# Values' product and output projection one step later, with every step's probabilities turned through memory

## The reference

```python
x = x + tanh(g_xattn[0]) * attention(layernorm(x), ctx)
x = x + tanh(g_ffn[0]) * (moe(layernorm(x)) + shared_ffn(layernorm(x)))

# attention: 32 query heads, 8 key/value heads, head size 128, per batch of 64 rows
q = rmsnorm(h @ Wq.T); k = rmsnorm(ctx @ Wk.T); v = ctx @ Wv.T
probs = softmax(q @ k.T / sqrt(128) + mask)
out = (probs @ v) @ Wo.T
# moe: 16 experts, the best two of each row
```

## Time and profile before

| | |
|---|---|
| median of 3 runs | 1366.95 us (1365.96 to 1368.43) |
| profiled execution | 1367.91 us |
| its span, first to last instruction | 1366.2 us |
| granted TensorE clock, mean | 0.999 |
| steps 4 to 55, from the start of step 4 to that of step 56 | 245.66 to 946.04 us |

### The profile page before, as it was taken

The page is one execution under the profiler, slowest core; times in us unless marked ns, Lnnn a source line. Parts: engine busy times, 40 slices in busy tenths (PEclk is TensorE's granted clock), DMA queues, the critical chain, the costliest instruction groups (busy, mean ns, idle before and its releaser), DMA issues.

```text
span 1366.2 us, 24589 instructions
## 1 busy us (share of the span) xinstructions
PE 1351.8 (99%) x8473; PEld 1092.8 (80%) x8474; DVE 1041.6 (76%) x2190; ACT 505.4 (37%) x1085; POOL 359.9 (26%) x375
## 2 busy tenths in 40 slices
PE   8999999999999999999999999999999999999998
PEld 7888877888888888888888888888887888777777
DVE  6676668898888888898988888888687655334459
ACT  4233244343434444344334343434344321222242
POOL 1122232212121221212121212122112100467746
PEclk9999999999999999999999999999999999999999
DMA  6766631222122221222121222212222344555548
GB/s 208 248 190 204 187 112 40 59 56 72 50 57 66 62 59 47 76 53 59 50 78 48 59 63 66 55 51 59 55 78 85 132 171 161 193 185 162 168 158 297
DMA packets 178209, 146.13 MB, mean 107 GB/s; under 512 B 77376, under 2 KB 139328, under 8 KB 177856
## 3 DMA queue, kind: packets, MB, share of 16 engines
q1 hardware_dynamic: 170592, 120.17, 29.4%
q0 software_dynamic: 7520, 24.65, 5.4%
HBM read 97.06 MB, written 47.71 MB: 106 GB/s over the span
## 4 chain that ended last, share of the span: by engine, by line
PE 80%; DVE 3%; issue 1%; DMA 0%; ACT 0%; POOL 0%; DVEq 0%; ACTq 0%
PE ps L677 20%; PE ps L679 19%; PE ps L678 19%; PE ps L1071 6%; PE ps L761 5%; PE ps L808 4%; PE ps L1087 3%; PE ps L1066 2%; PE ps L793 1%; DVE acc L2086 1%; DVE acc L2093 1%; PE ps L984 1%; PE ps L816 0%; PE ps L1118 0%; PE ps L769 0%
## 5 line engine op out<-in xcount | busy, mean ns | idle before, releaser
L574 POOL CAST vth<-vt 128x256 fp32r<-128x256 f32 x64 | 25.4, 397 | 538.6 <-PE ps L808 536.6
L1268 ACT CAST ah<-ps 128x256 fp32r<-128x256 f32 x256 | 83.1, 381 | 208.4 <-PE ps L679 202.0
L677 PE MATMUL ps<-hT,w0h 128*128 128x512 f32 x384 | 152.2, 396 | 1.2 <-DVE w0l L1542 1.2
L679 PE MATMUL ps<-hT,w0h 128*128 128x512 f32 x384 | 149.8, 390 | 0.0
L678 PE MATMUL ps<-hT,w0l 128*128 128x512 f32 x384 | 149.6, 390 | 0.0
L568 POOL TENSOR_TENSOR qr<-qv,mhalf 128x8 f32<-128x8 f32 x64 | 105.1, 1642 | 139.2 <-DVE qv L1672 113.5
L1228 ACT ACTIVATE qs<-ps,wqk 128x512 f32<-128x512 f32 x128 | 88.2, 689 | 125.8 <-PE ps L679 125.8
L1623 DVE TENSOR_TENSOR acc<-ps,acc 128x512 f32<-128x512 f32 x128 | 88.0, 687 | 50.5 <-PE ps L679 50.3
L677 PE MATMUL ps<-w0l,ah 128*128 128x512 f32 x256 | 105.9, 414 | 0.0
L1241 ACT ACTIVATE pb<-pb 128x256 f32<-128x256 f32 x128 | 48.3, 419 | 154.4 <-DVE pb L1692 154.4
L677 PE MATMUL ps<-w1l,ah 128*128 128x512 f32 x256 | 105.1, 411 | 0.0
(11 more groups left out here) (255 smaller groups left out, 3172.8 us busy)
## 6 DMA issues: line engine op xcount, KB each, us to landing
wraw<-in_w_att SPq DMA_DIRECT2D x64, 256.0 KB, 2.7
vbuf<-vo SPq DMA_DIRECT2D x16, 512.0 KB, 3.3
kbuf<-ko SPq DMA_DIRECT2D x16, 512.0 KB, 5.3
kt<-kbuf SPq DMA_DIRECT2D x128, 64.0 KB, 2.2
vt<-vbuf SPq DMA_DIRECT2D x64, 128.0 KB, 2.2
wgu<-in_w_gu SPq DMA_DIRECT2D x4, 2048.0 KB, 7.9
y<-ybuf SPq DMA_DIRECT2D x16, 512.0 KB, 6.9
pbuf<-pbT SPq DMA_DIRECT2D x26, 256.0 KB, 2.0
```

Of the source, the lines that this page charges most:

```text
L677: pe.matmul(dst, l_hi, r_lo, start=first, stop=False)
L679: return pe.matmul(dst, l_hi, r_hi, start=False, stop=last)
L1268: act.copy(ah[:, bp, :, b2, :], pv_view(bp, b2)).then_inc(a_hi, 1)
```

## The change

All steps from 2 to 56 now send their probabilities through memory; TensorE turns them only in steps 0 and 1 and in the last group. TensorE's step i computes `probs_v` of r = i-2 in place of i-1, and the projection follows it: second half of r-1, the small product of the sums, first half of r. The opening leaves out what step 2 did for r = 1, and step 56 (`catch_up`) does the products of two steps. The sums of squares of step 3 are made as those of steps 0 to 2 (`q_sums`). In odd steps VectorE now also turns `pb`; the rest of an even step's probabilities is made in the next odd step between the variance and the root, the rest of an odd step's at the end of that step, and the rest of an odd step's weight slice in the next even step between variance and root (`late`). SyncE's queue is written out: in odd steps keys, store, slice, values, `pt_raw`; in even steps store, `pt_raw`, values, slice.

```diff
-BY_DMA = (4, STEPS - NC)
-TURNED = (3, STEPS - NC + 1)
+BY_DMA = (2, STEPS - NC + 1)
+TURNED = (4, STEPS - NC + 1)
...
+            def probs_out(i):
+                sp.wait_ge(p_turned, i - BY_DMA[0] + 1)
+                if i > BY_DMA[0]:
+                    sp.wait_ge(p_back, 64 * (i - BY_DMA[0]))
+                sp.dma_start(pbuf, pbT[:].rearrange("p c m i -> p c (m i)")).then_inc(p_out, 16)
+
+            def probs_back(i):
+                sp.wait_ge(p_out, 16 * (i - BY_DMA[0] + 1))
+                sp.wait_ge(pT_evac, 2 * i)
+                for c in range(4):
+                    sp.dma_start(pt_raw[32 * c:32 * c + 32].rearrange("p q m i -> p q (m i)"),
+                                 p_ld[c]).then_inc(p_back, 16)
+
+            for i in range(STEPS - NC + 1):
+                if i % 2:
+                    sp.wait_ge(s_done, i + 1)
+                    load_k(i // 2 + 1)
+                if by_dma(i):
+                    probs_out(i)
+                if i == 0:
+                    load_v(1)
+                if i % 2 or not by_dma(i):
+                    load_slice(i)
+                if i % 2 and by_dma(i):
+                    load_v(i)
+                if by_dma(i):
+                    probs_back(i)
+                if i % 2 == 0 and by_dma(i):
+                    load_v(i)
+                    load_slice(i)
+            load_v(STEPS - NC + 1)
+
+            for t in range(1, NC - 1):
+                i = STEPS - NC + t
+                if t % 2:
...
             split_v(1)
-            split_v(2)
-            with pool.Fori(3, STEPS - 2) as j:
+            inverse_root(3)
+            with pool.Fori(4, STEPS - NC + 2) as j:
+                split_v(j - 2)
+                inverse_root(j)
...
+            def projected_0(r, w_o):
                 pe.wait_ge(a_hi, 4 * r + 6)
                 pe.wait_ge(a_lo, 4 * r + 6)
                 pe.wait_ge(acc_done, 2 * r + 2)
                 project_out(0, w_o, (0, 1, 2, 3))
...
+
+            def next_query(i):
+                if i % NC == NC - 1:
+                    pe.wait_ge(w_lo, i + 5)
+                for h in range(2):
+                    pe.wait_ge(q_sq, 2 * i + 1 + h)
+                    q_head(h, (i + 1) % 2, (i + 1) % NC // 2, att(i + 1)).then_inc(q_done, 1)
+
+            def step(i):
+
+                next_query(i)
+                probs_v(i - 2, i % 2)
+                scores((i + 1) // 2, (i + 1) % 2)
+                pe.wait_ge(acc_done, 2 * (i - 2) + 1)
+                project_out(1, att(i - 3), (0, 1, 2, 3))
+                if i + 1 == TURNED[0]:
+                    pe.wait_ge(const_dve, 6)
+                add_quarters(i + 1)
+                if i % NC == 2:
+                    pe.wait_ge(w_lo, i + 6)
+                projected_0(i - 2, att(i - 2))
+
+            def catch_up(i):
+
+                next_query(i)
+                probs_v(i - 2, 0)
+                scores((i + 1) // 2, (i + 1) % 2)
+                q_sums(i + 1)
+                pe.wait_ge(acc_done, 2 * (i - 2) + 1)
+                project_out(1, att(i - 3), (0, 1, 2, 3))
+                projected_0(i - 2, att(i - 2))
+                probs_v(i - 1, 1)
+                pe.wait_ge(acc_done, 2 * (i - 1) + 1)
+                project_out(1, att(i - 2), (0, 1, 2, 3))
+                projected_0(i - 1, att(i - 1))
...
+                last_step(i, o_ready=STEPS if i == STEPS - NC + 1 else None, last=(i == STEPS - 2))
...
+            def probs_hi(i, odd, bank=2):
+                if by_dma(i):
+                    act.wait_ge(p_back, 64 * (i - BY_DMA[0] + 1))
+                    act.wait_ge(pv_done, 2 * i + 2 - 2 * odd)
+                    act.copy(raw_view(0, odd), pt_raw[:]).then_inc(pT_hi, 2)
                     return
...
+            def act_step(i):
+
+                queries(i)
+                a_hi_tile(i - 2, 0)
+                if i % 2:
+                    probs_hi(i - 1, 0)
+                a_hi_tile(i - 2, 1)
+                split_slice(i, att(i + NC), i % NC)
+                exps(i + 1)
+                if i % 2:
+                    probs_hi(i, 1)
+
+            def act_catch_up(i):
+
+                queries(i)
+                a_hi_tile(i - 2, 0)
+                a_hi_tile(i - 2, 1)
+                split_slice(i, att(i + NC), i % NC)
+                exps(i + 1)
+                a_hi_tile(i - 1, 0)
+                a_hi_tile(i - 1, 1)
+                probs_hi(i, 0)
+
...
             def probs_lo(i, odd, bank=2):
-                if odd:
+                if by_dma(i):
+                    dve.wait_ge(pT_hi, 2 * i + 2)
+                    dve.tensor_tensor(raw_view(1, odd), pt_raw[:], raw_view(0, odd), ALU.subtract).then_inc(pT_evac, 2)
...
+            def turn_probs(i):
+                dve.wait_ge(p_ready, 2 * i + 2)
+                if i > BY_DMA[0]:
+                    dve.wait_ge(p_out, 16 * (i - BY_DMA[0]))
+                dve.transpose(pbT[:].rearrange("p c m i -> p (c m i)"),
+                              pb[:].rearrange("p (m z) (h j) -> p (z h) m j", z=2, h=2)).then_inc(p_turned, 1)
+
+            def dve_step(i):
+
+                odd = i % 2
+                late = i % 2 == 1 and 3 < i < STEPS - NC - 1
+                turn_probs(i)
+                turn_squares(i + 1, 0)
+                sum_squares(i + 1, 0)
+                if odd:
+                    slice_lo(i - 1, att(i + NC), i % NC - 1)
+                turn_squares(i + 1, 1)
+                sum_squares(i + 1, 1)
+                split_sums(i + 1)
+                a_rest(i - 2, 0)
+
+                def while_root():
+                    if odd:
+                        probs_lo(i - 1, 0)
+                    elif i > 4:
+                        slice_lo(i - 1, att(i - 1 + NC), (i - 1) % NC)
+                    add_out(2 * i - 3, 1, (2 * i - 5) % NT)
+                    a_rest(i - 2, 1)
+
+                def while_exp():
+                    add_out(2 * i - 2, 0, (2 * i - 4) % NT)
+
+                softmax(i + 1, while_root, while_exp, turn_before=i - BY_DMA[0] + 1)
                 if odd:
                     probs_lo(i, 1)
-                if turn:
-                    sum_squares(i + 1, 0)
-                    if odd:
-                        slice_lo(i - 1, w, sl - 1)
-                    turn_squares(i + 1, 1)
-                    sum_squares(i + 1, 1)
-                    split_sums(i + 1)
+                    if not late:
+                        slice_lo(i, att(i + NC), i % NC)
+
+            def dve_catch_up(i):
+
+                turn_probs(i)
+                a_rest(i - 2, 0)
+
+                def while_root():
+                    add_out(2 * i - 3, 1, (2 * i - 5) % NT)
+                    a_rest(i - 2, 1)
+
+                def while_exp():
+                    add_out(2 * i - 2, 0, (2 * i - 4) % NT)
+
+                softmax(i + 1, while_root, while_exp, turn_before=i - BY_DMA[0] + 1)
+                slice_lo(i, att(i + NC), i % NC)
+                a_rest(i - 1, 0)
+                add_out(2 * i - 1, 1, (2 * i - 3) % NT)
+                a_rest(i - 1, 1)
+                probs_lo(i, 0)
+                add_out(2 * i, 0, (2 * i - 2) % NT)
+
+            def dve_last(i, complete=(None, None)):
+
+                odd = i % 2
+                if odd:
...
+            for i in range(3, STEPS - NC):
+                dve_step(i)
```

More of the change, by code:

```diff
@@ L841, in outputs @@
                 project_out(0, w_o, (0, 1, 2, 3))
-            def step(d, odd, pair_q, w_q, w_before, w_o, q_ready=None, o_ready=None, last=False, turn=True):
-                i = 2 * d + odd
-                if q_ready is not None:
-                    pe.wait_ge(w_lo, q_ready)
+            def outputs(r, w_before, w_o, o_ready=None):
+                pe.wait_ge(acc_done, 2 * r + 1)
+                project_out(1, w_before, (0, 1, 2, 3))
+                if o_ready is not None:
+                    pe.wait_ge(w_lo, o_ready)
+                pe.wait_ge(pT_evac, 2 * r + 4)
+                projected_0(r, w_o)
@@ L869, in step @@
                     transpose_h2(3, 1)
-                dma = turn and by_dma(i, odd)
-                if not odd and not dma:
+                if i % 2 == 0:
                     pe.wait_ge(acc_done, 2 * i)
-                    transpose_probs(i, odd)
-                outputs(i - 1, w_before, w_o, o_ready, turn, dma)
+                    transpose_probs(i, 0)
+                outputs(i - 1, att(i - 2), att(i - 1), o_ready)
             for k in range(KD):
@@ L1273, in split_slice, with queries, act_last @@
                          w[0][:, sl * 512:(sl + 1) * 512], wraw[:]).then_inc(w_hi, 1)
-            def act_step(d, odd, w, sl):
-                i = 2 * d + odd
+            def queries(i):
+                act.wait_ge(s_done, i + 1)
+                for h in range(2):
+                    q_out(h, i + 1)
+                    squares(h, i + 1)
+            def act_step(i):
[6 more added lines that the diff above has]
+                exps(i + 1)
+                if i % 2:
```

(24 more changed lines are left out.)

207 lines of the change are left out of this document (56 added, 151 removed).

## The result

The changed kernel takes 1372.28 us (median of 6 runs, 1371.42 to 1373.45), the kernel before beside it 1366.57 (6 runs). The ratio is 1.0042, 95% interval 1.0032 to 1.0053: slower by 0.42%, 1.3 us above the upper end of the range. The profiled execution took 1372.0 us, its span is 4.0 us longer than before's (1370.2 against 1366.2), so my sum of -1.4 is off by 5.4. One execution of experiment 2, the one that was profiled, had a granted clock of 0.85 and took 1485.78 us; it is left out of the ratio there.

The account below looks back on a forecast made before the run. TensorE's own work, busy 99% of the span, was taken as the bound. -13.35 + 5.4 + 1.0 + 4.1 + 1.4 = -1.4 us gave a median of 1365.5 us, range 1359.5 to 1371.

Parts of the forecast that it names:

- my sum of -1.4: Whole kernel: the gain from removed turns and four losses together, -1.4 us against the kernel before.
- Turns gone, -13.35: TensorE, odd steps and steps 2 and 56: removed turns, less step 3's longer sums of squares, save 13.35 us without waits.
- The wait in even steps, 0.20: Even steps 4 to 56: TensorE waits 0.20 us for the odd step's probabilities, 27 times, +5.4 us.
- `ssg` to scaling is 2.44: VectorE's chain piece from the group sums to the scaling of the scores: 2.44 us, before it was 2.60.
- A: The small product of the sums, where the chain to the odd step's remaining probabilities starts; that chain was put at 8.60 us.
- SyncE's misses, +1.0: SyncE's loads and ScalarE's copies: with covers of 0.4 some come too late, +1.0 us (0 to 3, an estimate).
- the case that had a cover of 0.4: Even steps' slice lands 1.6 us into the next step; ScalarE copies it before the exponentials, by 2.2 against 2.6.
- The rival of late loads: SyncE's loads of an odd step's probabilities land too late, making the kernel slower, 1370 to 1376 us; chance 0.18.
- The opening, +4.1: Steps 3 and 4: TensorE waits 3.2 us at step 4's scores, 0.2 for the small product, 0.7 for the output's rest.
- The catch-up, +1.4: Step 56: the last projection half waits for the output's rest behind step 57's softmax, +1.4 us, from 0.5 to 3.
- The even-step wait doesn't come: VectorE's chain is 0.2 us shorter or partly overlaps, so even steps don't wait; 1357.5 to 1362 us, chance 0.22.
- VectorE the bound: VectorE bounds every step, by more than its cover of 0.25 us; 1366 to 1372 us, chance 0.08.

Follow-up runs that it names:

- experiment 2: The changed kernel with one head of the first projection half done ahead of the values' product in even steps; 1365.53 us, ratio 0.9991 to the kernel before.
- experiment 3: The changed kernel with VectorE's sum into `acc` put ahead of the operation with two SBUF operands; 1365.1 us, ratio 0.9993 to the kernel before.
- Experiment 5: The changed kernel with step 2's slice loaded before the probabilities' store, and the first half of `a` rounded before the catch-up's exponentials; 1369.14 us, ratio 1.0019.
- experiment 8: The changed kernel with the small product back between the projection's halves and the sum into `acc` first; 1376.04 us, ratio 1.0073 to the kernel before.
- all four edits together: The changed kernel with small product early, sum into `acc` first, slice's load first in the opening, rounding of `a` first in the catch-up; 1372.36 us, ratio 1.0043.

## Why the prediction was wrong

- **Turns gone, -13.35: right.** Odd steps last 13.22, as the even ones did; TensorE has 109 instructions less. (By the length of a turn as its price the sum would have been -31.5, not the -30.9 written there; nothing hangs on it.)
- **The wait in even steps, 0.20: the right place, the wrong size, and this is the step that failed.** It is 0.42 in every even step from 12 to 54, and 22 such steps times 0.22 are 4.8 of the 5.4 us that the sum is off. (Steps 4 to 55 take 698.9 us, 11.2 more than 52 steps of 13.225; the two terms for them, 5.4 less step 56's 0.2 and SyncE's 1.0, made 6.2.) The piece of the chain that was off is "`ssg` to scaling is 2.44", which measured 2.67. I had composed it of VectorE's starts alone and written of the moved rests that they "lie in GpSimd's root, which VectorE waited out anyway". They don't lie in it, they start ahead of it and lengthen it by 0.37, and then the root is the longer way: 0.63 from `ssg` to its start (711.10 to 711.73), 2.01, 0.03 of handover.

  The longer root costs more than the difference to my 2.44, for other pieces were off too and hid part of it. VectorE's own way from `ssg` to scaling is 2.32, as 3 has it (705.39 to 707.71): the operation behind `qv` starts before `qv` ends, which I had added end to start. A to `ssg` is 0.23 (710.87 to 711.10), not 0.37, and from the rest of the probabilities to TensorE it is 0.14 (705.21 and 0.68 to 706.03), not 0.04. The whole chain is 0.23 + 2.67 + 5.08 + 0.68 + 0.14 = 8.80 against 8.39 of TensorE's, a wait of 0.41. With a root of 1.64 it would be 8.45 and the wait 0.06, which is about by how much the even step of experiment 3 is longer than the odd one (13.28 and 13.23). So 0.35 of the 0.41 is the longer root, and without it my 0.20 would have been too high. The prediction did name 2.60 as the upper end of this piece, +9.7 in place of +5.4, but its range kept too little of that: the 4.3 more on 1365.5 are 1369.8, and 1371 leaves 1.2 for all the rest.
- **SyncE's misses, +1.0: right in kind, 1.5 in size.** Steps 5, 8 and 9 last 13.85 to 13.87, together 1.5 more than their like later on. In steps 5 and 9 the weight slice of the even step lands late, the case that had a cover of 0.4: ScalarE copies it 2.28 and 2.82 us into the step (1.3 to 2.2 in the other odd steps from 7 on), the exponentials stand behind the copy, and VectorE's `sm` waits for them. In step 9 the slice stands in SyncE's queue behind a store of the probabilities (issued at 303.73) that took 4.2 us to land, where the median is 2.0:

```profile
313.33 0.62 ACT L1300 CAST w0h<-wraw 128x512 fp32r<-128x512 f32 x1 [5.02 <-DMA wraw<-in_w_att]
```

```profile
259.90 0.69 DVE L1738 TENSOR_REDUCE sm<-pb 128x8 f32<-128x512 f32 x1 [0.53 <-ACT pb L1269]
...
314.61 0.69 DVE L1738 TENSOR_REDUCE sm<-pb 128x8 f32<-128x512 f32 x1 [0.75 <-ACT pb L1269]
```

  In step 9 that makes the output's rest late, and TensorE waits 0.41 for it. In step 5 a collision comes on top. `w1l` normally starts 0.01 ahead of GpSimd's `vtl`; here, a little late, it starts 0.07 behind it and takes 1.21 instead of 0.68:

```profile
263.53 0.73 POOL L589 TENSOR_TENSOR vtl<-vt,vth 128x256 fp32r<-128x256 f32 x1
```

```profile
263.60 1.21 DVE L1760 TENSOR_TENSOR w1l<-wraw,w1h 128x512 fp32r<-128x512 f32 x1
```

```profile
267.36 0.47 PE L695 MATMUL ps<-w0l,ah 128*128 128x512 f32 x1 [0.41 <-issue]
```

  The 0.2 of step 8 go with two set-up operations that VectorE has in that step alone (0.22 and 0.48 us); step 8 of the kernel before has them too and is 0.14 longer than its like. The profile puts no wait of TensorE in steps 4 to 55 down to a DMA: the late load reaches it through ScalarE and VectorE. The rival of late loads was about others, those of the odd steps' probabilities, and it didn't come: neither ScalarE nor VectorE waits for `pt_raw`.
- **The opening, +4.1: right.** Waits of 3.11, 0.54 and 0.35 are 4.00; I had 3.2, 0.2 and 0.7. Experiment 5 confirms the chain (slice behind probabilities) and shows that the keys stand behind it.
- **The catch-up, +1.4: right.** 1.22, and 5 takes it away.
- **The rivals.** "The even-step wait doesn't come" needed a chain 0.2 shorter; it is 0.2 longer, 8.80 against 8.60. "VectorE the bound" isn't the changed kernel, but it is experiment 8. The case that came was in none of them: VectorE's operation makes another engine's longer. A sum of mean durations doesn't show that, but the trace of the kernel before had one case of it, the only root of 2.02 among its 64, in the last group, with a `w0l` 0.17 us ahead of it:

```profile
1041.01 0.69 DVE L1720 TENSOR_TENSOR w0l<-wraw,w0h 128x512 fp32r<-128x512 f32 x1
```

```profile
1041.18 2.02 POOL L568 TENSOR_TENSOR qr<-qv,mhalf 128x8 f32<-128x8 f32 x1 [1.43 <-DVE qv L1663]
```

Three of the 26 even steps between 4 and 55 (4, 6 and 10) have no wait at the values' product. The rows say why: each follows a step (3, 5 and 9) in which TensorE waited for the output's rest behind A. From A to the start of the next step it then needs 3.44 to 3.48 in place of 2.85, while in step 5 `ssg` is only 0.22 later (0.45 behind A), so there a chain of 9.02 meets 9.02 of TensorE's.

## What to carry to other kernels

When an operation is moved beside another engine's, don't only ask whether it fits in that engine's time: ask whether it changes that time. Here 0.37 us on an operation that nobody edited turned a change from a tie into a loss, and to exchange two lines took 7 us back. And price such a chain as the longest of its ways at each join (VectorE's own pieces, GpSimd's root), since they lay 0.02 us apart here (2.32 and 2.30). Look for the odd one out of a constant duration, too: the one root of 2.02 in the old trace was the warning. Two cures of the same wait needn't add up: an operation that fills a wait in one order is pushed behind it in another.

## What the runs showed of the hardware

- A VectorE operation of 128x512 with both operands in SBUF, started 0.16 to 0.17 us ahead of GpSimd's root on 128x8, makes the root 2.01 us long instead of 1.64; the four kernels without it there (before, 3, 8 and all four edits together) have a mean of 1642 ns, those with it 1948 to 1961. Started 0.44 behind the root's start it is not slowed and doesn't slow the root. The sum into `acc`, with one operand in PSUM, started 0.16 ahead of the root in experiment 3, and the root took 1.64.
- Against GpSimd's longer `vtl` (128x256, two SBUF operands, 0.73 by itself) it goes both ways. `vtl` 0.07 ahead: VectorE's operation takes 1.21 in place of 0.68. `vtl` 0.01 behind, in step 39: it takes 1.28 in place of 0.73.

```profile
720.91 1.28 POOL L589 TENSOR_TENSOR vtl<-vt,vth 128x256 fp32r<-128x256 f32 x1
```

- In all three cases the one that comes second is longer by 0.12 to 0.14 less than what the first had left to run: `w1l` by 0.53 of 0.66, `vtl` by 0.55 of 0.67, the root by 0.37 of 0.51.

The rule of the Trainium skill named above (SBUF — State Buffer, SBUF: two separate sides) says that the one that starts first holds the ports and the other fully blocks. The trace agrees in these three cases, but for the 0.12 to 0.14. It doesn't agree where VectorE's operation starts behind the root's start: nothing was held there, with some 1.2 us of the root left, and there the measurement decides.
